# Block-wise matmuls for the last two doubling steps of a triangular inverse

## The chip, the cores and the metric

The kernel runs on one core of a Trainium2 chip, in one launch. Its time is the device time in microseconds (us); each kernel is run several times and the median is compared. The engines named below are TensorE (PE; its weight loads are listed as PEld), VectorE (DVE), ScalarE (ACT), GpSimd (POOL) and the DMA queue of SyncE (SP).

## The reference

A transformer layer over 16 batches of 128 tokens with 512 channels: cross attention to a context of 2048 rows, a gated delta-rule memory layer, and a mixture of 16 experts. The change lies in the second part. For each batch and each of 4 heads (head width 128) the tokens are cut into two chunks of 64, and

```python
strict = jnp.tril(jnp.ones((C, C), bool), -1)
A0 = -jnp.where(strict, jnp.einsum('bnid,bnjd->bnij', wk, wk) * L[:, None], 0.0)
A = jnp.linalg.inv(eye - A0)          # C = 64
...
def step(S, inp):
    v_corr = A_i @ v_i
    wk_corr = A_i @ wk_i
    v_new = v_corr - wk_corr @ S
    o_i = rkg_i @ S + intra_i @ v_new
    S = gamma_C * S + wkg_i @ v_new
```

With two chunks and a state that starts at zero, the kernel treats each head as one 128x128 unit lower triangular system and inverts that.

## The kernel before

One batch after the other goes through the core. A batch's attention is 64 units (4 groups of heads by 16 key blocks), and a unit has two ticks, so a batch has TICKS = 128 ticks. Every engine's program is written out by the same loop over batches `i` and ticks `t`: at each tick it emits a score matmul (L460, every second tick), matmuls whose row maxima are wanted (L447), transposes of the context (L412), products with the values (L472), and the pieces of other batches that the tables place at this tick. So the order on an engine is fixed by hand; an engine that waits holds up everything behind it.

`finish(b, t)` is the part of batch b that comes after its attention and runs while batch b+1 is in attention: output projection, second layer norm, the memory layer, routing. The table `LEVEL_AT` gives three ticks for each of six levels of the inverse. `MT` is the strictly triangular matrix (held transposed, in the buffer x1), `X` the inverse so far (buffer xn2) and `XT` its transpose (buffer xr), each 128x512: four heads side by side. The profile prints these buffers as x, xn and xr. Level lv joins blocks of size s = 2 << lv into blocks of 2s:

- at LEVEL_AT[lv][0] PE computes MT' X into the bank (per head 128x128x128), and DVE copies it to `Y`, masked by a constant `C_LEVEL + lv` that keeps only the s x s blocks that join (L974, buffer Y)
- at LEVEL_AT[lv][1] PE computes Y' XT (per head), and DVE subtracts it from `XT` (L988)
- at LEVEL_AT[lv][2], for all levels but the last, PE transposes XT (L616) and ACT copies it to `X` (L793).

The last level (lv = 5, s = 64) has a form of its own before the change: the helper `joining` multiplies only rows and columns of the 64x64 block (L426), and DVE copies (L979) or subtracts (L988) only that block. Levels 0 to 4 multiply the full 128x128 of each head (L420, helper `per_head`). Every matmul here has 4-byte operands, and the profile lists each of them as two MATMUL records, so four heads are eight records.

Between these steps PE works on attention: L452 transposes the 4 columns of row maxima `mneg` that DVE made in L887. GpSimd adds up the exponentials of every unit (L1094, 60 in a batch) and computes the small reciprocal square roots of the norms (L1097 to L1101); `sums` (L494) needs its additions of a whole batch. The last batch (b = 15) has no attention beside it: its levels are cut into four one-head parts in four banks, and small filler matmuls (L479) stand between its steps.

Of the kernel before, what the change touches and what calls it, by code (L numbers as in the profile page):

```python
# [8 lines left out]
ALU, ACT, AX = mybir.AluOpType, mybir.ActivationFunctionType, mybir.AxisListType  # L9

P = 128
# [6 lines left out]
CH = 64  # L18
# [13 lines left out]
LAST = B - 1  # L32
WARM = {-1: 14, 14: 4}
LEVELS = 6

# [88 lines left out]
def attention(nc, T, w1_first, w1_in):  # L126
    with ExitStack() as ctx:
# [29 lines left out]
        def chunk(b, c):  # L157
# [18 lines left out]
        xr, x1, xn2, x12, rk, V, Y, turned = (  # L176
            sb(n, [P, D]) for n in ("xr", "x1", "xn2", "x12", "rk", "V", "Y", "turned"))
# [3 lines left out]
        XT, MT, X, IT, Vn = xr, x1, xn2, rk, Y  # L181
# [51 lines left out]
        y_dve, xt_dve, x_act = count("y_dve", LEVELS), count("xt_dve", LEVELS), count("x_act", LEVELS - 1)  # L233
# [71 lines left out]
        def heads(ap, n=DH):  # L305
            return ap.rearrange("p (h t) -> p h t", h=n)
# [97 lines left out]
        def _(e):  # L404
# [18 lines left out]
            def joining(out, lhs, rhs, hs):  # L423

                for h in hs:
                    ins = e.matmul(out[:, h, :], lhs[:, h, :], rhs[:, h, :], start=True, stop=True)  # L426
                return ins
# [118 lines left out]
            def finish(b, t):  # L546
# [3 lines left out]
                if t in POST["x1"]:  # L550
# [5 lines left out]
                    ins = project(x1_bank(b), turned, wo, c)  # L556
# [13 lines left out]
                if t in POST["V"]:  # L570
                    ins = project(P_BANK, turned, ww, POST["V"].index(t))
# [19 lines left out]
                for lv in range(LEVELS):  # L591
                    if t == LEVEL_AT[lv][0]:
                        if b == LAST and lv == 0:
                            busy(4)
                        for i, bk, hs in parts:
                            e.wait_ge(*(x_act.at(*level(b, lv - 1, i)) if lv else post_act.at(b, "X1")))
                            if lv < LEVELS - 1:
                                ins = per_head(bk, lambda h: cut(MT, h), lambda h: cut(X, h), hs)
                            else:
                                ins = joining(heads(bk[:])[CH:P, :, 0:CH], heads(MT[:])[0:CH, :, CH:P],  # L600
                                              heads(X[:])[0:CH, :, 0:CH], hs)
                            ins.then_inc(y_pe.sem, 1)
                    if t == LEVEL_AT[lv][1]:
                        for i, bk, hs in parts:
                            e.wait_ge(*y_dve.at(*level(b, lv, i)))
                            if lv < LEVELS - 1:
                                ins = per_head(bk, lambda h: cut(Y, h), lambda h: cut(XT, h), hs)
                            else:
                                ins = joining(heads(bk[:])[0:CH, :, CH:P], heads(Y[:])[CH:P, :, 0:CH],
                                              heads(XT[:])[CH:P, :, CH:P], hs)  # L610
                            ins.then_inc(z_pe.sem, 1)
                    if t == LEVEL_AT[lv][2] and lv < LEVELS - 1:
                        for i, bk, hs in parts:
                            e.wait_ge(*xt_dve.at(*level(b, lv, i)))
                            for h in hs:
                                ins = e.transpose(bk[:, h * P:(h + 1) * P], cut(XT, h), ident)  # L616
                            ins.then_inc(xt_pe.sem, 1)
# [247 lines left out]
        def _(e):  # L865
# [71 lines left out]
            def finish(b, t):  # L937
                banks = banks_of(b)
                w = D // len(banks)
                nh = DH // len(banks)  # L940
# [27 lines left out]
                for lv in range(LEVELS):  # L968
                    if t == LEVEL_AT[lv][0]:
                        for i, bk in enumerate(banks):  # L970
                            cols = slice(i * w, (i + 1) * w)
                            e.wait_ge(*y_pe.at(*level(b, lv, i)))
                            if lv < LEVELS - 1:
                                e.tensor_tensor(  # L974
                                    heads(Y[:, cols], nh), heads(bk[:, cols], nh),
                                    cst[:, C_LEVEL + lv, :].unsqueeze(1).to_broadcast([P, nh, P]), ALU.mult).then_inc(
                                    y_dve.sem, 1)
                            else:
                                e.tensor_copy(heads(Y[:, cols], nh)[CH:P, :, 0:CH],  # L979
                                              heads(bk[:, cols], nh)[CH:P, :, 0:CH]).then_inc(y_dve.sem, 1)  # L980
                    if t == LEVEL_AT[lv][1]:
                        for i, bk in enumerate(banks):
                            cols = slice(i * w, (i + 1) * w)
                            e.wait_ge(*z_pe.at(*level(b, lv, i)))
                            xt, z = XT[:, cols], bk[:, cols]
                            if lv == LEVELS - 1:
                                xt, z = heads(xt, nh)[0:CH, :, CH:P], heads(z, nh)[0:CH, :, CH:P]
                            e.tensor_tensor(xt, xt, z, ALU.subtract).then_inc(xt_dve.sem, 1)  # L988
                if t == POST["x2_add"]:
                    e.wait_ge(*late_pe.at(b, "x2"))  # L990
                    if b:
# [424 lines left out]
```

## Time and profile before

| | |
|---|---|
| time, median of 3 runs | 2172.67 us (2171.48 to 2175.91) |
| time of the profiled execution | 2173.11 us |
| its span | 2171.3 us |
| PE busy | 2095.7 us, 97% |
| POOL busy | 1635.7 us, 75% |
| DVE busy | 1272.3 us, 59% |
| ACT busy | 1220.7 us, 56% |
| mean granted TensorE clock | 0.986 of full speed |

The page gives each engine's busy time and share of the span. A matmul record's end is modelled and reaches past the start of the next one, so PE's 97% does not say that it streams all the time: the distance from one record's start to the next one's is the better measure. The attention part with everything around it lasts to about 1746 us of the span, the experts fill the rest.

### The profile page before, as it was taken

The numbers are of one execution on the slowest core, as the hardware profiler recorded it, in microseconds if no ns is written. First come the engines' busy times: TensorE is split into PE (matmuls) and PEld (weight loads), VectorE is DVE, ScalarE is ACT, GpSimd is POOL, SyncE is SP. The second block draws the span as 40 slices with busy tenths as digits, with TensorE's granted clock in tenths as the row PEclk, the third lists the DMA queues.
The fourth block names the chain that finished last, engine by engine and source line by source line (L and its number), as shares of the span: only waits on it lengthen the run. The fifth ranks groups of instructions, "written<-read, shape, count | busy, mean of one in ns | idle before, by whom it ended". The sixth has DMA issues, their size and how long they took to land. (4 is left out here: it accounts for less than half of the span.)

```text
span 2171.3 us, 35745 instructions
## 1 busy us (share of the span) xinstructions
PE 2095.7 (97%) x12908; PEld 1421.6 (65%) x12908; DVE 1272.3 (59%) x2226; ACT 1220.7 (56%) x2277; POOL 1635.7 (75%) x1387
## 2 busy tenths in 40 slices
PE   7879999999999999999999999999989999999999
PEld 5436565656565656666565656565645789999998
DVE  5656767676666666676767676766664433333332
ACT  3756575666666566666665666666655233433333
POOL 0778888888888888888888888889798145555555
PEclk8989999999999999999999999999999999999999
DMA  4752121212212121212131212112200089999994
GB/s 159 242 113 90 48 74 45 73 52 66 75 48 74 45 73 53 74 44 82 39 97 43 74 43 74 59 57 71 79 15 11 12 313 357 363 352 359 360 348 177
DMA packets 107055, 262.31 MB, mean 121 GB/s; under 512 B 8960, under 2 KB 34304, under 8 KB 98688
## 3 DMA queue, kind: packets, MB, share of 16 engines
q1 hardware_dynamic: 96912, 234.92, 31.6%
q10 hardware_dynamic: 6384, 14.62, 2.3%
q0 software_dynamic: 3584, 10.49, 1.2%
q8 instruction: 103, 1.69, 0.3%
q14 instruction: 72, 0.59, 0.1%
HBM read 223.67 MB, written 25.72 MB: 115 GB/s over the span
## 5 line engine op out<-in xcount | busy, mean ns | idle before, releaser
L1094 POOL TENSOR_TENSOR psum<-psum,weights 128x512 f32<-128x512 f32 x896 | 1152.6, 1286 | 163.4 <-ACT weights L702 60.5
L880 DVE TENSOR_REDUCE mpart<-bank 128x1 f32<-128x512 f32 x1024 | 680.4, 684 | 308.9 <-PE bank L447 300.0
L702 ACT ACTIVATE weights<-bank 128x512 f32<-128x512 f32 x1024 | 597.0, 599 | 324.1 <-PE bank L460 313.3
L460 PE MATMUL bank<-qT,kT 97*128 97x512 f32 x1024 | 482.8, 477 | 10.0 <-DMA qT<-mrow 6.5
L447 PE MATMUL bank<-kT,qT 96*128 96x512 f32 x1024 | 450.0, 451 | 9.6 <-DVE mpart L880 6.8
L447 PEld LDWEIGHTS bank<-kT,qT 96*128 96x128 f32 x1024 | 196.9, 192 | 141.2 <-issue 87.4
L1346 POOL TENSOR_TENSOR w2l<-w,w2h 128x1024 fp32r<-128x1024 f32 x64 | 202.9, 3171 | 75.8 <-PE ebank L1259 54.5
L460 PEld LDWEIGHTS bank<-qT,kT 97*128 97x128 f32 x1024 | 195.7, 193 | 89.4 <-issue 49.2
L472 PE MATMUL bank<-weights,v 128*32 128x512 f32 x2048 | 251.3, 609 | 0.0
L737 ACT COPY w_first<-bank 128x512 f32<-128x512 f32 x248 | 144.7, 584 | 67.6 <-PE bank L412 64.6
L1289 ACT ACTIVATE hh<-ebank 128x512 fp32r<-128x512 f32 x64 | 38.2, 597 | 224.6 <-PE ebank L1243 224.6
L412 PE MATMUL bank<-cst,w_first 128*128 128x128 f32 x992 | 151.5, 276 | 8.3 <-ACT w_first L737 4.7
L412 PEld LDWEIGHTS bank<-cst,w_first 128*128 128x128 f32 x992 | 119.9, 141 | 51.8 <-issue 22.2
L1283 ACT CAST w2h<-w 128x2048 fp32r<-128x2048 f32 x64 | 121.5, 1898 | 43.8 <-DMA w<-in_w 43.8
L472 PEld LDWEIGHTS bank<-weights,v 128*32 128x32 f32 x2048 | 53.7, 110 | 120.2 <-issue 93.8
L538 PE MATMUL bank<-w_first,wkv 128*64 128x512 f32 x512 | 124.0, 605 | 0.0
L1315 DVE SCALAR_TENSOR_TENSOR hl<-ebank,hh 128x512 fp32r<-128x512 f32 x64 | 44.2, 691 | 133.6 <-ACT hh L1289 133.6
L1243 PE MATMUL ebank<-dT,w_first 128*128 128x128 f32 x1024 | 120.2, 278 | 0.9 <-DVE dT L1304 0.9
L1243 PEld LDWEIGHTS ebank<-dT,w_first 128*128 128x128 f32 x1024 | 119.3, 195 | 2.4 <-issue 1.2
L1310 DVE TENSOR_TENSOR w2l<-w,w2h 128x1024 fp32r<-128x1024 f32 x64 | 79.1, 1235 | 71.1 <-PE ebank L1259 48.0
L1243 PEld LDWEIGHTS ebank<-dT,w 128*128 128x128 f32 x1024 | 117.5, 192 | 1.4
L1243 PE MATMUL ebank<-dT,w 128*128 128x128 f32 x1024 | 118.2, 275 | 0.0
(174 smaller groups left out, 3019.3 us busy)
## 6 DMA issues: line engine op xcount, KB each, us to landing
w<-in_w SPq DMA_DIRECT2D x48, 2048.0 KB, 19.9
w_first<-in_ctx SPq DMA_DIRECT2D x62, 1024.0 KB, 5.2
w_first<-in_w SPq DMA_DIRECT2D x16, 2048.0 KB, 12.2
dispatched<-route ACTq DMA_DIRECT2D x17, 513.0 KB, 8.5
dis<-dispatched SPq DMA_DIRECT2D x16, 513.0 KB, 3.5
qT<-qh SPq DMA_DIRECT2D x128, 64.0 KB, 3.4
qT<-qs SPq DMA_DIRECT2D x64, 64.0 KB, 2.1
xr<-in_x SPq DMA_DIRECT2D x16, 256.0 KB, 2.7
```

Source lines behind the costliest of these rows:

```text
L412: ins = e.transpose(out[0:m, j * P:(j + 1) * P], src(j), ident)
L447: e.matmul(a[:], qT[b % 2][0:3 * HD, (4 * g + h) * P:(4 * g + h + 1) * P], kT[b % 2][0:3 * HD, c * 512:(c + 1) * 512], start=True, stop=Tr ...
L460: e.matmul(B_BANK[u % 2][:], kT[b % 2][0:3 * HD + 1, k * P:(k + 1) * P], qT[b % 2][0:3 * HD + 1, g * 512:(g + 1) * 512], start=True, stop= ...
L472: ins = e.matmul(PV_BANK[HD * j:HD * (j + 1), :], v1[b % 2][:, k + j, :], p[(UNITS * b + u + j) % NP], start=k == 0, stop=k == KB - 4)
L538: ins = e.matmul(KV_BANK[rows, :], wkv[:, j, :], cxT[c % 2][:, j, :], start=j < 2, stop=j >= 2)
L702: e.activation(p[n % NP], B_BANK[u % 2][:], ACT.Exp).then_inc(p_act.sem, 1)
L737: e.copy(cxT[c % 2][:, :, kk * P:(kk + 1) * P], turn_bank(b, ("t", k))[:].rearrange("p (c t) -> p c t", c=DC)).then_inc(cxT_act.sem, 1)
L880: e.tensor_reduce(mpart[g % 2][:, 4 * (n % 4) + n // 4:4 * (n % 4) + n // 4 + 1], max_bank(b, g, n)[:], AX.X, ALU.max).then_inc(max_dve.se ...
L1094: e.tensor_tensor(acc[:], first, p[(UNITS * b + u) % NP], ALU.add).then_inc(psum_pool.sem, 1)
L1243: ins = e.matmul(H_BANK[g][:, f * P:(f + 1) * P], w1[q][:, c, (4 * g + f) * P:(4 * g + f + 1) * P], dT[q][:, c, :], start=c == 0, stop=c = ...
L1283: e.copy(w2h[g][:], w2[q][:, 4 * g:4 * g + 4, :]).then_inc(w2h_act.sem, 1)
L1346: e.tensor_tensor(w2l[g % 2][:, 2:4, :], w2[q][:, 4 * g + 2:4 * g + 4, :], w2h[g][:, 2:4, :].bitcast(F32), ALU.subtract).then_inc(w2l_pool ...
```

## The change

Level 4 (s = 32) gets the same treatment as level 5: `joined(lv)` lists the places of the blocks. For level 5 there is one, rows 0 to 63 with 64 to 127, as before. For level 4 there are two, (0 to 31 with 32 to 63) and (64 to 95 with 96 to 127), so each head's 128x128x128 matmul becomes two 32x32x32 matmuls, and each DVE instruction over 128 partitions and 512 columns becomes two over 32 partitions and 4x32 columns. The masked multiply becomes a plain copy. `Y` and `XT` outside the blocks are neither written nor read in these steps. Levels 0 to 3 and the transposes are unchanged. One semaphore increment follows the last of the two, as one followed the single instruction.

```diff
+BLOCKS = 4
+def joined(lv):
+    n = 2 << lv
+    return [(slice(a, a + n), slice(a + n, a + 2 * n)) for a in range(0, P, 2 * n)] if lv >= BLOCKS else []
...
-                            if lv < LEVELS - 1:
+                            if lv < BLOCKS:
                                 ins = per_head(bk, lambda h: cut(MT, h), lambda h: cut(X, h), hs)
-                            else:
-                                ins = joining(heads(bk[:])[CH:P, :, 0:CH], heads(MT[:])[0:CH, :, CH:P],
-                                              heads(X[:])[0:CH, :, 0:CH], hs)
+                            for up, low in joined(lv):
+                                ins = joining(heads(bk[:])[low, :, up], heads(MT[:])[up, :, low],
+                                              heads(X[:])[up, :, up], hs)
...
-                            if lv < LEVELS - 1:
+                            if lv < BLOCKS:
                                 ins = per_head(bk, lambda h: cut(Y, h), lambda h: cut(XT, h), hs)
-                            else:
-                                ins = joining(heads(bk[:])[0:CH, :, CH:P], heads(Y[:])[CH:P, :, 0:CH],
-                                              heads(XT[:])[CH:P, :, CH:P], hs)
+                            for up, low in joined(lv):
+                                ins = joining(heads(bk[:])[up, :, low], heads(Y[:])[low, :, up],
+                                              heads(XT[:])[low, :, low], hs)
...
-                            else:
-                                e.tensor_copy(heads(Y[:, cols], nh)[CH:P, :, 0:CH],
-                                              heads(bk[:, cols], nh)[CH:P, :, 0:CH]).then_inc(y_dve.sem, 1)
+                            for j, (up, low) in enumerate(joined(lv)):
+                                ins = e.tensor_copy(heads(Y[:, cols], nh)[low, :, up],
+                                                    heads(bk[:, cols], nh)[low, :, up])
+                                if j == len(joined(lv)) - 1:
+                                    ins.then_inc(y_dve.sem, 1)
...
-                            if lv == LEVELS - 1:
-                                xt, z = heads(xt, nh)[0:CH, :, CH:P], heads(z, nh)[0:CH, :, CH:P]
-                            e.tensor_tensor(xt, xt, z, ALU.subtract).then_inc(xt_dve.sem, 1)
+                            if lv < BLOCKS:
+                                e.tensor_tensor(xt, xt, z, ALU.subtract).then_inc(xt_dve.sem, 1)
+                            for j, (up, low) in enumerate(joined(lv)):
+                                part = heads(xt, nh)[up, :, low]
+                                ins = e.tensor_tensor(part, part, heads(z, nh)[up, :, low], ALU.subtract)
+                                if j == len(joined(lv)) - 1:
+                                    ins.then_inc(xt_dve.sem, 1)
```

On PE, the order around level 4 of a middle batch, before the change (xn,x are the operands X and MT; xr,Y are XT and Y; the L616 row is the transposes of level 4):

```order
L420 MATMUL bank<-xn,x 128x128 x4
L460 MATMUL bank<-qT,kT 128x512
L452 MATMUL bank<-cst,mneg 128x128
L460 MATMUL bank<-qT,kT 128x512
L447 MATMUL bank<-kT,qT 128x512
L420 MATMUL bank<-xr,Y 128x128 x4
L460 MATMUL bank<-qT,kT 128x512
L447 MATMUL bank<-kT,qT 128x512
L616 MATMUL bank<-cst,xr 128x128 x4
```

And the same place with the change; its lines stand 9 further down in the file:

```order
L435 MATMUL bank<-xn,x 32x32 x8
L469 MATMUL bank<-qT,kT 128x512
L461 MATMUL bank<-cst,mneg 128x128
L469 MATMUL bank<-qT,kT 128x512
L456 MATMUL bank<-kT,qT 128x512
L435 MATMUL bank<-xr,Y 32x32 x8
L469 MATMUL bank<-qT,kT 128x512
L456 MATMUL bank<-kT,qT 128x512
L625 MATMUL bank<-cst,xr 128x128 x4
```

Nothing moved; the two groups of four became groups of eight smaller matmuls, and everything between them is the same. On DVE, the same stretch before (L880 finds row maxima of the L447 matmuls):

```order
L887 TENSOR_REDUCE mneg<-mpart 128x4
L974 TENSOR_TENSOR Y<-bank,cst 128x512
L880 TENSOR_REDUCE mpart<-bank 128x1
L988 TENSOR_TENSOR xr<-xr,bank 128x512
L880 TENSOR_REDUCE mpart<-bank 128x1 x3
L979 COPY Y<-bank 64x4x64
```

And with the change:

```order
L896 TENSOR_REDUCE mneg<-mpart 128x4
L988 COPY Y<-bank 32x4x32 x2
L889 TENSOR_REDUCE mpart<-bank 128x1
L1001 TENSOR_TENSOR xr<-xr,bank 32x4x32 x2
L889 TENSOR_REDUCE mpart<-bank 128x1 x3
L988 COPY Y<-bank 64x4x64
```

Each of the two DVE instructions of level 4 became two, at the same place. ACT, POOL and the DMA queues issue what they issued before, in the same order.

## Rows read from the trace of the kernel before

**Rows 1.** Busy time of each engine in one batch's stretch (window, length, engines, clock, DMA).
```profile
404.80:507.20 102.40, 100.62 (x611) 62.15 (x610) 69.60 (x125) 66.05 (x134) 87.69 (x81) 1.00 0.20 63
```

**Rows 2.** Timeline, PE around level 4 of one batch (start, us, what, idle before).
```profile
431.24 1.16 PE L420 MATMUL bank<-xn,x 128*128 128x128 f32 x8 [0.20 <-ACT xn L793]
...
432.15 0.48 PE L460 MATMUL bank<-qT,kT 97*128 97x512 f32 x1
...
432.50 0.49 PE L460 MATMUL bank<-qT,kT 97*128 97x512 f32 x1
...
432.82 0.40 PE L447 MATMUL bank<-kT,qT 96*128 96x512 f32 x1
...
433.18 1.16 PE L420 MATMUL bank<-xr,Y 128*128 128x128 f32 x8
...
434.10 0.48 PE L460 MATMUL bank<-qT,kT 97*128 97x512 f32 x1
...
434.41 0.40 PE L447 MATMUL bank<-kT,qT 96*128 96x512 f32 x1
...
435.12 0.66 PE L616 MATMUL bank<-cst,xr 128*128 128x128 f32 x4 [0.31 <-DVE xr L988]
```

**Rows 3.** Timeline, DVE in the same stretch.
```profile
431.88 0.17 DVE L887 TENSOR_REDUCE mneg<-mpart 128x4 f32<-128x16 f32 x1
432.44 0.69 DVE L974 TENSOR_TENSOR Y<-bank,cst 128x512 f32<-128x512 f32 x1 [0.39 <-PE bank L420]
433.26 0.69 DVE L880 TENSOR_REDUCE mpart<-bank 128x1 f32<-128x512 f32 x1
434.38 0.69 DVE L988 TENSOR_TENSOR xr<-xr,bank 128x512 f32<-128x512 f32 x1 [0.43 <-PE bank L420]
```

**Rows 4.** Timeline, PE at level 4 of the next batch.
```profile
533.64 1.16 PE L420 MATMUL bank<-xn,x 128*128 128x128 f32 x8 [0.20 <-ACT xn L793]
...
537.52 0.66 PE L616 MATMUL bank<-cst,xr 128*128 128x128 f32 x4 [0.30 <-DVE xr L988]
```

**Rows 5.** Timeline, PE at the first matmuls of level 5, same batch as rows 2.
```profile
436.32 0.39 PE L447 MATMUL bank<-kT,qT 96*128 96x512 f32 x1
436.64 0.67 PE L426 MATMUL bank<-xn,x 64*64 64x64 f32 x8
437.24 0.50 PE L460 MATMUL bank<-qT,kT 97*128 97x512 f32 x1
```

**Rows 6.** Groups by shape: busy us, mean ns of one, idle before.
```profile
L420 PE MATMUL bank<-xn,x 128*128 128x128 f32 x640 | 89.3, 282 | 3.7 <-ACT xn L793 3.2 <-ACT xn L787 0.4
L974 DVE TENSOR_TENSOR Y<-bank,cst 128x128 f32<-128x128 f32 x20 | 4.8, 291 | 5.0 <-PE bank L420 5.0
```

**Rows 7.** One line's instructions, L426: ns min/median/max.
```profile
L426 PE MATMUL bank<-xn,x x128: 218/218/267, 231.9 to 1722.5; 64*64 64x64 f32 x128
```

**Rows 8.** Timeline, DVE at level 4 of the last batch.
```profile
1719.81 0.96 DVE L974 TENSOR_TENSOR Y<-bank,cst 128x128 f32<-128x128 f32 x4 [0.67 <-PE bank L420]
```

**Rows 9.** Timeline, PE, a window 0.06 us long at products with values.
```profile
458.78 0.64 PE L472 MATMUL bank<-weights,v 128*32 128x512 f32 x4
```

**Rows 10.** Timeline, PE at the transposes of level 4, batch 14.
```profile
1655.94 0.66 PE L616 MATMUL bank<-cst,xr 128*128 128x128 f32 x4 [0.55 <-DVE xr L988]
```

**Rows 11.** Timeline, POOL beside level 4, same batch as rows 2.
```profile
430.60 5.52 POOL L1094 TENSOR_TENSOR psum<-psum,weights 128x512 f32<-128x512 f32 x4 [1.19 <-ACT weights L702]
```

**Rows 12.** Timeline, GpSimd's last addition of a batch and the sums that need it.
```profile
462.67 1.27 POOL L1094 TENSOR_TENSOR psum<-psum,weights 128x512 f32<-128x512 f32 x1
...
465.24 0.16 PEld L494 LDWEIGHTS bank<-psum,cst 128*32 128x32 f32 x8 [0.17 <-POOL psum L1094]
```

**Rows 13.** Timeline, POOL at the third norm of one batch.
```profile
451.69 0.19 POOL L1097 TENSOR_TENSOR rs<-mv,eps 128x1 f32<-128x1 f32 x1 [0.30 <-DVE rs L935]
```

**Rows 14.** Timeline, POOL at the second norm of the next batch.
```profile
479.50 1.54 POOL L1094 TENSOR_TENSOR psum<-psum,weights 128x512 f32<-128x512 f32 x1
481.84 0.19 POOL L1097 TENSOR_TENSOR rs<-mv,eps 128x1 f32<-128x1 f32 x1 [0.80 <-DVE rs L935]
```

More of the change, by code:

```diff
@@ L972, in finish @@
                             e.wait_ge(*y_pe.at(*level(b, lv, i)))
-                            if lv < LEVELS - 1:
+                            if lv < BLOCKS:
                                 e.tensor_tensor(
@@ L985, in finish @@
                             xt, z = XT[:, cols], bk[:, cols]
-                            if lv == LEVELS - 1:
-                                xt, z = heads(xt, nh)[0:CH, :, CH:P], heads(z, nh)[0:CH, :, CH:P]
-                            e.tensor_tensor(xt, xt, z, ALU.subtract).then_inc(xt_dve.sem, 1)
+                            if lv < BLOCKS:
+                                e.tensor_tensor(xt, xt, z, ALU.subtract).then_inc(xt_dve.sem, 1)
[4 more added lines that the diff above has]
+                                    ins.then_inc(xt_dve.sem, 1)
                 if t == POST["x2_add"]:
```

## The prediction

> **What bounds the kernel now.** I read the busy times first: PE is busy for 97% of the span. The window of one batch shows the same on a smaller scale [rows 1]: in 102.40 us PE is busy for 100.62, POOL for 87.69, DVE for 69.60, ACT for 66.05, at the full granted clock. The neighbour batch repeats it to the hundredth: its level 4 begins at 533.64 [rows 4], 102.40 us after that of its predecessor at 431.24 [rows 2]. So one stretch of 102.4 us, looked at closely, stands for nearly the whole attention part, and what it loses or saves counts about 14 times.
>
> The second view is the timeline of PE at level 4 [rows 2]. A record's modelled end overlaps the next start, so I read distances of starts. From the first product of level 4 (431.24) to its transposes (435.12) pass 3.88 us. In them PE issues two groups of eight 128x128 records, each followed by the next instruction 0.91 to 0.92 us after it began, and five matmuls of attention. Two places are not filled with work. Two matmuls of 512 columns follow each other 0.31 to 0.34 us apart, but 0.71 us pass from L447 at 434.41 to the transposes at 435.12, and the row names the wait: DVE's subtraction L988. The second group (433.18) starts 0.36 after L447, with DVE's multiply just done at 433.13. In the DVE view [rows 3] the pieces join end to end: PE's first group ends at 432.40, DVE works from 432.44 to 433.13, PE from 433.18 to 434.34, DVE from 434.38 to 435.07, PE goes on at 435.12. Each hand-over costs 0.04 to 0.06 us. So at level 4 this chain, not the sum of PE's work, sets the pace, and all other engines follow PE.
>
> **The change part by part.** It shortens four links of that chain and moves nothing else.
>
> PE's records. Eight 128x128 records last 1.16 us from first start to last end [rows 2]; a record lasts 0.28 [rows 6], so they start (1.16 - 0.28)/7 = 0.126 us apart on average. Level 5's eight 64x64 records last 0.67 us [rows 5], one lasts 0.218 [rows 7], so they start (0.67 - 0.22)/7 = 0.064 us apart. Half the size, half the spacing. No row shows a 32x32 record. From below I bound its spacing by the values products: four 32-column records that use different columns of the array end within 0.64 us of the first start [rows 9], hardly longer than one alone, so issue itself costs next to nothing. From above, by the 0.064 of the nearest shape. The straight line through 128 and 64 columns gives 0.033 for 32, and I take it, since these matmuls halved with size once already. Sixteen records then take 15 x 0.033 = 0.50 from first to last start, and a last record of about 0.19 (0.28, 0.22, then 0.03 to 0.05 less). I add 0.02 for the step to the second block: first start to last end 0.71, against 1.16.
>
> The way out of small tiles. Behind level 5's group L460 starts 0.60 after the first start [rows 5], 0.15 after the last record's start (0.45). So behind 16 small records PE goes on 0.52 + 0.15 = 0.67 after the group's start, against 0.91. The way in: from L447 (436.32) to level 5's group (436.64) are 0.32 us [rows 5], where such a matmul otherwise holds PE for about 0.23; I charge 0.32.
>
> The Trainium skill speaks against the step: TensorEngine Tiling, section Performance Considerations, says that a matmul over 1 column takes as long as one over 60, and TensorE: Matmul & The Clock Gate, section Back-to-back issue gap, gives about 62 ns a matmul where the sequencer's firmware decodes. With the latter the sixteen records would fill 0.99 us and the groups would gain nothing; that is priced as a rival below, from rows. The records of different columns [rows 9] do not agree with such a floor.
>
> DVE. Level 4's multiply and subtraction take 0.69 us each [rows 3]. Two instructions over 4x32 = 128 columns replace each. The trace has them over 128 columns in the last batch: 0.291 us for one [rows 6], and four of them in 0.96 [rows 8], so (0.96 - 0.29)/3 = 0.223 apart. Two take 0.223 + 0.291 = 0.51, 0.18 less. That they use 32 partitions instead of 128 I count as nothing.
>
> Now the new timeline, from the same start 431.24. PE's group ends at 431.95. DVE is not free: L887 ends at 432.05 [rows 3] and stands ahead, so the copies run from 432.08 to 432.60. PE meanwhile goes on at 431.91 with L460, L452, L460 and L447. By the distances of today (0.35 from L460 to L460, 0.32 to L447 [rows 2]) the L447 starts at 432.58 and the second group 0.32 later, at 432.90. DVE's result was there at 432.65, so the wait for DVE is gone and PE's own work decides: 0.28 us gained so far. The second group ends at 433.61. DVE's reduction L880 belongs to L447 and stands ahead of the subtraction; it starts 0.44 after L447 today and lasts 0.69, so it now runs from 433.02 to 433.71. The subtractions follow, until 434.24 at the latest, and PE's transposes start at 434.25 to 434.30, or up to 0.08 earlier if DVE overlaps the two. PE's own work would have allowed 432.90 + 0.67 + 0.33 + 0.23 = 434.13. I take 434.24 against 435.12: **0.88 us less per batch.** So the chain still decides at the transposes, with a wait of 0.1 instead of 0.5.
>
> How often. Batches 0 to 13 have this form (14 x 0.88 = 12.3). Batch 14 has no row maxima beside it and waits even longer for L988 (0.55, [rows 10]): another 0.9. In the last batch each of four one-head parts gets two DVE instructions of 32 columns for one of 128. Four DVE instructions take 0.96 there today [rows 8]; eight short ones, at 0.10 to 0.12 apart, take about as long. PE's first result comes 0.1 to 0.15 earlier and the way to the transposes gets shorter by about 0.3. Sum: 12.3 + 0.9 + 0.3 = 13.5 us.
>
> Is the gain kept? Everything behind is relative to PE's stream, except where POOL falls behind. POOL waits for ACT until 430.60 [rows 11], just ahead of level 4, and then adds without a pause; that start does not move with the saving of its own batch. PE's `sums` need its last addition of the batch, which ends at 463.94; L494 starts at 465.24 [rows 12]. The row names POOL as what it waited for, but POOL had been done for 1.30 us, so that much is spare. The third norm waits 0.30 for DVE [rows 13], and at the second norm of the next batch POOL, busy until 481.04, waits 0.80 [rows 14]: together 1.1 us spare, more than 0.88. After that POOL waits for ACT again. So the gain is kept, with about 0.2 us left before POOL would bind. A gain of 1.2 us or more per batch would not be kept whole.
>
> The sum against the profiled execution: 2173.1 - 13.5 = 2159.6; the median of the runs lies 0.4 under that execution, so **2159.2 us**.
>
> **The rivals.**
> - The spacing does not fall below that of 64x64 (an issue floor). With p the spacing, PE's stream from the first group to the transposes is 30p + 1.9 us (twice 0.15 out, 0.32 in, the attention matmuls 0.35 + 0.32 + 0.33 + 0.23, the rest of the step between blocks). At p = 0.060 to 0.064 that is 3.7 to 3.8, and with the slower chain about 3.75 against 3.88: 0.1 to 0.15 a batch, 2 us in all, 2171. For it: no row shows a smaller record. Against: spacing halved from 128 to 64 columns, and records in different columns start at once.
> - POOL takes part of the gain: if its additions slow, or if the spare at the norms can't be used since ACT needs POOL's result earlier, only 0.3 to 0.6 a batch stays: 2164 to 2168.
> - Slower: small tiles of the same rows and columns can't load weights under a running matmul, so a record costs as long as its 64x64 weight load or more, 0.13 us. Then PE's stream is 30 x 0.13 + 1.9 = 5.8 us against 3.88, 1.9 more per batch, 2201. Breakeven is p = 0.066, and 0.2% slower (0.3 a batch) begins at p = 0.076. Against it: the 64x64 records stand 0.064 apart with four heads on one tile, and a quarter of the array should not be worse.
> - Nothing: the wait moves whole to the next place, such as level 5's first product, which today starts right behind PE's work [rows 5]. It waits for ACT's copy, which follows the transposes and so comes earlier too; I see nothing there that stands still.
>
> **How the numbers follow.** My forecast (0.7 to 1.1 a batch, 2155 to 2163): 0.72. Partly kept, or a spacing between 0.04 and 0.055 (2163 to 2168): 0.12. The floor, or nothing (2168.4 to 2177): 0.10. Slower than that: 0.06. A measurement can tell about 0.2% (4.3 us) from no change. Faster by more 0.84, within it 0.10, slower 0.06. The range for 8 in 10 reaches from 2154, all of POOL's spare used (1.2 a batch), into the partly kept case: 2168.
>
> **What would show it.** In the profile after: 32x32 records at a mean of about 0.19 us, sixteen of them from first to last start in 0.5 us; a distance of about 3.0 us from the first product of level 4 to its transposes in place of 3.88; DVE's copies of 32 partitions right behind L887; batches 101.5 us apart; POOL's wait ahead of the second norm down to about 0.1. I am wrong if the sixteen records take 0.9 us or more, if the distance shrinks and the batches stay 102.4 apart (then look for the engine that the saving ran into, POOL first), or if two DVE instructions over 32 partitions take more than 0.6.

## The result: slightly slower, with its saving visible in the trace

The changed kernel took 2177.25 us (median of 19 runs, 2173.43 to 2181.89), the kernel before 2171.59 beside it (19 runs, 2169.18 to 2179.06). The ratio is 1.0024, with a 95% interval of 1.0016 to 1.0032. The forecast of 2159.2 us and its range to 2168 were wrong. The profiled execution of the changed kernel took 2179.65 us, its span is 2177.8, and its mean granted clock 0.984 (before: 2171.3 and 0.986). Three executions among the runs reported below fell into a disturbed state of 3410 us or more and are left out of their medians.

I start with the page of the kernel after: the busy times, the granted clock in 40 slices, then the window of one batch, which answers to [rows 1].

```profile
PE 2091.4 (96%) x13164; PEld 1410.0 (65%) x13164; DVE 1274.1 (59%) x2264; ACT 1221.7 (56%) x2277; POOL 1636.8 (75%) x1387
...
PEclk8999999999999999999999999999998999999999
```

```profile
401.20:503.60 102.40, 100.02 (x626) 61.36 (x625) 69.47 (x127) 66.10 (x133) 87.73 (x81) 1.00 0.21 63
```

The busy times hardly differ from those before. The clock row has an 8 late in the span (slice 31), where the row before has a 9: PE had less than its full clock there for a while, and I return to it. To see whether the change did what it says, I go to its place. This is the timeline of PE and then of DVE around level 4 in a middle batch after the change (start, us, what, idle before), against [rows 2, 3].

```profile
428.67 0.59 PE L435 MATMUL bank<-xn,x 32*32 32x32 f32 x16 [0.20 <-ACT xn L802]
429.19 0.49 PE L469 MATMUL bank<-qT,kT 97*128 97x512 f32 x1
...
430.26 0.59 PE L435 MATMUL bank<-xr,Y 32*32 32x32 f32 x16
...
431.12 0.40 PE L456 MATMUL bank<-kT,qT 96*128 96x512 f32 x1
...
431.60 0.65 PE L625 MATMUL bank<-cst,xr 128*128 128x128 f32 x4
```

```profile
429.51 0.59 DVE L988 COPY Y<-bank 32x128 f32<-32x128 f32 x2
430.37 0.69 DVE L889 TENSOR_REDUCE mpart<-bank 128x1 f32<-128x512 f32 x1 [0.27 <-PE bank L456]
430.98 0.56 DVE L1001 TENSOR_TENSOR xr<-xr,bank 32x128 f32<-32x128 f32 x2
```

From the first product (428.67) to the transposes (431.60) pass 2.93 us in place of 3.88: 0.95 less. The sixteen records take 0.59 from the first start to the last end. PE no longer waits for DVE ahead of the second group; ahead of the transposes it still does, but less: they start 0.48 after L456 in place of 0.71, 0.06 after the end of DVE's subtractions. Yet the next batch shows the same pace as before:

```profile
531.06 0.31 PE L435 MATMUL bank<-xn,x 32*32 32x32 f32 x4 [0.20 <-ACT xn L802]
```

That is 102.39 us after 428.67; before it was 102.40 [rows 2, 4]. So each batch saves 0.95 us at level 4 and gives it back elsewhere. I followed PE forward from the transposes until the two traces were level again. The place is PE's transposes of the next batch's x, at tick 101 (`xnt` of the table of preparations), just before a batch ends. First the kernel before, not shown so far, then the kernel after: all engines, only the rows that form the chain.

```profile
430.60 9.79 POOL L1094 TENSOR_TENSOR psum<-psum,weights 128x512 f32<-128x512 f32 x7 [1.19 <-ACT weights L702]
...
440.34 0.20 POOL L1097 TENSOR_TENSOR rs<-mv,eps 128x1 f32<-128x1 f32 x1
...
441.24 0.19 POOL L1101 TENSOR_TENSOR rs<-rs 128x1 f32<-128x1 f32 x1
441.41 1.05 PE L420 MATMUL bank<-V,xr 128*128 128x128 f32 x8
441.53 0.81 ACT L717 ACTIVATE xin<-xin,rs 128x512 f32<-128x512 f32 x1
442.40 0.44 PE L412 MATMUL bank<-cst,xin 128*128 128x128 f32 x2
```

```profile
428.04 9.80 POOL L1109 TENSOR_TENSOR psum<-psum,weights 128x512 f32<-128x512 f32 x7 [1.17 <-ACT weights L711]
...
438.69 0.19 POOL L1116 TENSOR_TENSOR rs<-rs 128x1 f32<-128x1 f32 x1
...
438.92 0.81 ACT L726 ACTIVATE xin<-xin,rs 128x512 f32<-128x512 f32 x1 [0.92 <-POOL rs L1116]
439.79 0.66 PE L421 MATMUL bank<-cst,xin 128*128 128x128 f32 x4 [0.83 <-ACT xin L726]
```

Read each block backwards. PE's transposes of xin need ACT's normalisation, that needs POOL's reciprocal square root (three small instructions, L1097 to L1101, after the change L1112 to L1116), and those stand in POOL's queue behind seven additions. The additions began ahead of level 4 (430.60 and 428.04, where ACT still set POOL's pace) and ran without a pause for 9.8 us. So from POOL's first addition to PE's transposes of xin pass 442.40 - 430.60 = 11.80 us before and 439.79 - 428.04 = 11.75 after, whatever PE saves in between. Before, this chain of POOL and ACT and PE's own work arrived nearly together: the group L420 started 0.99 before the transposes, where the like groups of level 4 hold PE for 0.91 to 0.92 [rows 2], and the row names no wait. So there was no time to spare at this place. After, PE stands still for 0.83 us and ACT for 0.92, and the gain is gone. From level 4's transposes to those of xin it is 7.28 us before (435.12 to 442.40) and 8.19 after (431.60 to 439.79): 0.91 of 0.95 given back.

The loss has other places: the last batch and the clock around batches 14 and 15. This is DVE and then PE at level 4 of the last batch after the change (DVE's row before is in [rows 8]).

```profile
1721.41 1.67 DVE L988 COPY Y<-bank 32x32 f32<-32x32 f32 x8 [0.61 <-PE bank L435]
1723.12 1.59 DVE L1001 TENSOR_TENSOR xr<-xr,bank 32x32 f32<-32x32 f32 x8
```

```profile
1721.12 0.68 PE L435 MATMUL bank<-xn,x 32*32 32x32 f32 x16
...
1723.54 1.70 PE L625 MATMUL bank<-cst,xr 128*128 128x128 f32 x4 [0.15 <-DVE xr L1001]
1725.17 1.01 PE L435 MATMUL bank<-xn,x 64*64 64x64 f32 x7
...
1732.41 3.67 PE L425 MATMUL bank<-wr,turned 128*128 128x512 f32 x8
...
1767.28 0.47 PE L1272 MATMUL ebank<-w2h,hh 128*128 128x512 f32 x1 [3.23 <-POOL w2l L1361]
```

And the same place before:

```profile
1719.36 1.08 PE L420 MATMUL bank<-xn,x 128*128 128x128 f32 x8
...
1721.98 0.75 PE L426 MATMUL bank<-xn,x 64*64 64x64 f32 x8
...
1727.38 3.67 PE L416 MATMUL bank<-wr,turned 128*128 128x512 f32 x8
```

Level 4 of the last batch takes 4.05 us after (1721.12 to 1725.17) and 2.62 before. Nothing runs beside it, so DVE sets the pace, and eight small copies take 1.67 where four whole multiplies took 0.96. (The last rows of the two blocks, products with `wr` and, after the change, a product of the experts, serve below.)

Last, windows over stretches at half clock, of before (its second row, at full clock, is the place of a stretch of after) and after (length; busy us of PE, PEld, DVE, ACT, POOL with their instructions; granted clock; DMA share; GB/s).

```profile
1675.20:1682.00 6.80, 6.79 (x28) 3.03 (x27) 1.06 (x6) 2.47 (x8) 6.08 (x6) 0.50 0.00 0
...
1724.00:1731.00 7.00, 6.97 (x40) 4.87 (x39) 0.00 (x0) 1.17 (x2) 0.00 (x0) 1.00 0.00 0
...
1747.00:1757.10 10.10, 8.31 (x37) 7.94 (x38) 0.69 (x1) 0.33 (x1) 0.00 (x0) 0.50 0.95 332
```

```profile
1652.50:1659.00 6.50, 6.50 (x32) 2.39 (x31) 0.43 (x1) 2.51 (x5) 5.26 (x5) 0.50 0.01 3
1672.90:1686.40 13.50, 13.50 (x56) 8.50 (x60) 2.80 (x13) 3.92 (x9) 11.45 (x11) 0.50 0.01 3
...
1724.10:1730.70 6.60, 6.30 (x34) 5.42 (x35) 2.16 (x11) 1.46 (x5) 0.00 (x0) 0.50 0.00 0
...
1768.40:1771.70 3.30, 3.30 (x10) 2.53 (x9) 0.41 (x1) 1.90 (x1) 2.07 (x1) 0.50 1.01 405
```

And PE at the transposes of batch 14's level 4 after, which answers to [rows 10]:

```profile
1651.70 0.66 PE L625 MATMUL bank<-cst,xr 128*128 128x128 f32 x4 [0.23 <-DVE xr L1001]
```

Around the last two batches, before the change, PE is at 0.5 of full speed (the 1.2 GHz level) for one stretch of 6.8 us; after it, for three, 26.6 us together. Where the experts begin it is the other way round: 10.1 us before, 3.3 after.

With these rows the two spans can be reckoned. At the level 4 shown above the kernel after is already 2.57 us ahead (431.24 against 428.67). That can't be put down to the change, since the start of the program takes more or less from execution to execution: three variants of the experiments below, which have whole blocks up to this batch like the kernel before, reach the same place at 429.37, 429.73 and 434.39. At the transposes of batch 14's level 4 the kernel after is 4.24 ahead (1655.94 against 1651.70), and at the last batch's level 4 it is 1.76 behind (1721.12 against 1719.36): 6.0 lost between them, where it has 20.0 us at half clock and the kernel before 6.8. Half of these 13.2 more is 6.6. Level 4 itself costs 1.43 more. From level 5's start to the products with `wr` pass 5.40 before and 7.24 after: 1.84 lost, in the stretch at half clock. From there to the end of the span pass 443.92 (2171.3 - 1727.38) and 445.39 (2177.8 - 1732.41): 1.47 more. -4.24 + 6.0 + 1.43 + 1.84 + 1.47 = 6.5, the difference of the spans.

The 1.47 don't belong to level 4 of the last batch. Two variants below with whole blocks there take 445.4 and 445.7 from the same place to the end, and the variant with small blocks there alone takes 443.7. What differs is where the half clock falls. Before, the stretch of 10.1 us lies where PE waits for the experts' weights in any case: from PE's first instruction of the experts to the first product with w2 pass 14.39 us there (1747.91 to 1762.30), and 14.55 after the change at full clock (1752.73 to 1767.28), the last 3.23 of them a wait. After, the stretch of 3.3 us falls on products that nothing holds up: they start 0.43 apart in it and 0.23 outside.

### The profile page after: what moved, and what is told of

Its sections match the earlier page's. It is cut to its first block and busy times, and to the rows that moved or that the text cites. A ratio compares the mean times of both kernels' runs of the same rounds, so it can differ in the third digit from the quotient of the medians.

```text
span 2177.8 us, 36295 instructions
## 1 busy us (share of the span) xinstructions
PE 2091.4 (96%) x13164; PEld 1410.0 (65%) x13164; DVE 1274.1 (59%) x2264; ACT 1221.7 (56%) x2277; POOL 1636.8 (75%) x1387
## 5 line engine op out<-in xcount | busy, mean ns | idle before, releaser
L456 PE MATMUL bank<-kT,qT 96*128 96x512 f32 x1024 | 448.8, 449 | 9.7 <-DVE mpart L889 6.7
L456 PEld LDWEIGHTS bank<-kT,qT 96*128 96x128 f32 x1024 | 196.5, 192 | 140.4 <-issue 88.0
```

Source lines behind the costliest of these rows:

```text
L456: e.matmul(a[:], qT[b % 2][0:3 * HD, (4 * g + h) * P:(4 * g + h + 1) * P], kT[b % 2][0:3 * HD, c * 512:(c + 1) * 512], start=True, stop=Tr ...
```

## The experiments

My theories after the result: **A**, POOL's backlog at the first norm of the next batch takes the gain of the middle batches. **B**, in the last batch, two DVE instructions for one cost time, and the clock follows. The rivals: the small matmuls themselves cost PE something elsewhere, or the gain is bounded by another engine than POOL. Every run stands beside runs of the kernel before on the same chip.

### Which batches carry the loss

Two kernels, in which `joined` and the tests on `BLOCKS` depend on the batch:

```diff
-BLOCKS = 4
+def blocks(b):
+    return 4 if b < LAST else 5      # e1_not_last
+    return 5 if b < LAST else 4      # e2_last_only
```

Of the first, the small blocks in batches 0 to 14, was expected:

> The small blocks at level 4 for batches 0 to 14 only; the last batch keeps the full 128x128 products and the single DVE instructions. Theory A (the 0.95 us that a middle batch gains at level 4 is given back 5 us later, where PE's transposes of the next batch's x wait for ACT, and ACT for POOL; the loss of the whole change comes from the last batch): 0 to 3 us below the kernel before, batches 102.4 us apart. Rival B (the loss comes from the middle batches or batch 14, whose PE works less and loses clock): 4 to 7 us above the kernel before, as the whole change. Rival C (a mere difference between builds, such as the start of the run): no relation to which batches are changed.

Of the second, the small blocks in the last batch alone:

> The small blocks at level 4 in the last batch only. Theory A: 4 to 7 us above the kernel before; level 4 of the last batch takes about 4.1 us from its first product to level 5's first in place of 2.6, and a stretch at half clock follows it. Rival B: within 1.5 us of it, the 1.5 us of the longer level 4 alone at most.

Measured beside 2174.64 for the kernel before (23 runs): the first 2175.26 (11 runs), ratio 0.9997 [0.9989, 1.0006]; the second 2178.54 (12 runs), ratio 1.0017 [1.0008, 1.0026]. So the change in fifteen batches together comes to nothing that can be told from zero (the interval is about 2 us to either side), and most of the loss is that of the one last batch. What the profile of the kernel after lost around batch 14 does not appear in the median of the first kernel, though its own profiled execution, the slowest of the eleven (2178.42), has stretches of 6.7 and 13.5 us there too. In the second kernel DVE's eight copies in the last batch take 1.67 us, as in the kernel after, and level 4 takes 4.05. A stretch at half clock comes here too, as level 4 ends:

```profile
1726.30:1733.00 6.70, 6.39 (x36) 5.98 (x37) 1.61 (x8) 1.09 (x3) 0.00 (x0) 0.50 0.00 0
```

From level 5's start (1726.72) to the products with `wr` (1734.28) pass 7.56 us in place of 5.40. So 1.43 for level 4 and 2.16 for the clock behind it make 3.6; the timed runs lose 3.9 (2178.54 against 2174.64).

### Moving the place where the gain is lost

If the wait for POOL's norm takes the gain, a later place for what needs it should set the gain free. In the table of preparations (ticks relative to the batch's start) I moved ACT's normalisation and PE's transposes seven ticks back, with the change and without it:

```diff
-STEADY = Prep(norm=-32, xn=-29, xnt=-27,
+STEADY = Prep(norm=-32, xn=-22, xnt=-20,
```

> The changed kernel, with ACT's normalisation of the next batch's x moved 7 ticks later (xn -29 to -22) and PE's transposes of it with it (xnt -27 to -20), so that POOL's backlog has some 5 us more before anyone waits for it. Theory A: the 0.95 us per middle batch stays: batches 101.5 us apart, 12 to 13 us less in the middle than in the kernel with the same move and without the small blocks (next run), so with the last batch's loss 6 to 9 us less than it in all. Rival D (PE's stream or another link fixes 102.4): batches stay 102.4 apart in both.

> The kernel before with the same two table entries moved. Theory A: about as the kernel before, 0 to 3 us less (the 0.1 us that PE waits there per batch goes), batches 102.3 to 102.4 apart. Rival D: the same. If this alone gains 10 us, the wait at x was worth more than I read and level 4 was bound by it both ways.

Measured: with the change 2190.56 (6 runs, 2181.23 to 2198.79), ratio 1.0079 [1.0054, 1.0104]; without it 2190.26 (5 runs, 2188.16 to 2192.04), ratio 1.0072 [1.0059, 1.0085]. The move is bad in itself: without the change it was expected to cost nothing, and it costs 15.6 us. At the new place PE waits for ACT anyway, as the row without the change shows:

```profile
449.39 0.66 PE L412 MATMUL bank<-cst,xin 128*128 128x128 f32 x4 [1.07 <-ACT xin L717]
```

Batches are 103.55 us apart without the change and 102.55 with it, so under the same move the change is worth 1.00 us per batch, and the profiled spans are 2188.0 and 2179.4. The medians are equal all the same, where 6 to 9 us less were expected: three of the six executions with the change took 2181 to 2184 us at a mean clock of 0.982, the other three 2197 to 2199 at 0.973 to 0.975. The saving is there, and the clock takes it back in half of the executions. These two runs support A by the distances of their batches, not by their times.

### Giving POOL's norm an earlier place

The better edit leaves ACT and PE where they are and puts the statistics and POOL's three small instructions four ticks earlier, ahead of more of its additions. One number changes, again with the change and without:

```diff
-STEADY = Prep(norm=-32, xn=-29, xnt=-27,
+STEADY = Prep(norm=-36, xn=-29, xnt=-27,
```

> The changed kernel with one table entry moved: the statistics and GpSimd's reciprocal root of the next batch's x come 4 ticks earlier (norm -32 to -36), which puts GpSimd's three small instructions ahead of two of its additions; ACT's and PE's parts stay where they were. Theory A (the gain is given back because PE's transposes of x wait for ACT and ACT for POOL's backlog): PE no longer waits there, and batches are 101.4 to 101.7 us apart in place of 102.4. The tail's loss stays, and clock may be lost more often. Rival D (something else than POOL fixes 102.4): 102.4 as before.

> The kernel before with the same entry moved. Theory A: batches 102.3 to 102.4 apart, since PE waited for only 0.1 us there, and a time within 3 us of the kernel before. Rival D: the same here; what tells is the difference to the run above, 0.8 to 1.0 us per batch by theory A, none by D.

Measured beside 2174.20 (34 runs): with the change 2168.83 (10 runs), ratio 0.9981 [0.9966, 0.9996]; without it 2172.19 (10 runs), ratio 1.0003 [0.9989, 1.0017]. These two runs decide A. The same edit is worth nothing to the kernel before, where PE arrived together with POOL's chain, and it releases the gain in the kernel after. The rows, with the change in a later batch (POOL, ACT and PE, then the x transposes of the next batch), and without it:

```profile
529.02 6.96 POOL L1109 TENSOR_TENSOR psum<-psum,weights 128x512 f32<-128x512 f32 x5 [1.18 <-ACT weights L711]
...
536.83 0.19 POOL L1116 TENSOR_TENSOR rs<-rs 128x1 f32<-128x1 f32 x1
539.07 0.81 ACT L726 ACTIVATE xin<-xin,rs 128x512 f32<-128x512 f32 x1
539.93 0.66 PE L421 MATMUL bank<-cst,xin 128*128 128x128 f32 x4
...
641.49 0.66 PE L421 MATMUL bank<-cst,xin 128*128 128x128 f32 x4
```

```profile
542.14 0.66 PE L412 MATMUL bank<-cst,xin 128*128 128x128 f32 x4
...
644.55 0.44 PE L412 MATMUL bank<-cst,xin 128*128 128x128 f32 x2
```

POOL's small chain now stands behind five additions instead of seven and ends 2.05 us before ACT starts with it, and neither ACT nor PE waits. With the change the batches are 101.56 us apart (641.49 - 539.93), without it 102.41. The difference, 0.85 a batch, is what I had forecast (0.88) as the change's own gain. No other engine took it back: the rival that something else than POOL bounds the batch falls.

### The early norm without the last batch, and without the last two

The small blocks in batches 0 to 14, with norm=-36, and then in batches 0 to 13 (`4 if b < LAST - 1 else 5`), which leaves out batch 14 as well:

> Small blocks for batches 0 to 14, the last batch as before, and norm 4 ticks earlier: both causes of loss taken away. Theory A: 10 to 13 us less than the kernel before when the clock holds, 2160 to 2166. If the clock falls in more of the executions (as in half of those of the run with x moved 7 ticks), the times spread over 10 us or more and the median is worse.

> Small blocks for batches 0 to 13 only, norm 4 ticks earlier. Theory G (the small blocks of batch 14, where no row maxima fill PE, are what makes the half clock after it last 13.7 us in place of 6.8): 6.8 us of half clock there and 3 us less than the run with batches 0 to 14, 2160 or so. Rival H (the length of that stretch follows from the phase at which the attention ends, not from batch 14's blocks): 13.7 us again, and the same time as that run.

The first: 2162.99 (11 runs, 2161.42 to 2167.91), ratio 0.9959 [0.9946, 0.9971]. Without the last batch the kernel with the early norm gains another 5.8 us (2168.83 to 2162.99), somewhat more than the price of that batch alone (3.9). The second: 2161.41 (6 runs, 2159.79 to 2166.86) beside 2172.29 (16 runs), ratio 0.9953 [0.9938, 0.9969]. It is the fastest version measured, ahead of both kernels; its lead over the first is within the intervals, as the two were timed beside different runs of the kernel before.

Their profiles (spans 2161.2 and 2158.0) differ in the clock around batch 14. A window of the first, and one of the second:

```profile
1661.20:1674.70 13.50, 12.85 (x56) 8.50 (x60) 2.81 (x13) 4.70 (x11) 11.92 (x12) 0.50 0.01 1
```

```profile
1660.10:1666.70 6.60, 6.60 (x31) 3.45 (x29) 1.06 (x6) 2.95 (x7) 5.88 (x6) 0.50 0.00 0
```

With small blocks in batch 14 the half clock lasts 13.5 us, with whole ones 6.6, worth up to about 3.4 us. From level 4 of batch 14 to that of the last batch pass 69.4 us in the first (1640.30 to 1709.74) and 67.2 in the second (1637.35 to 1704.57). The spans differ by 3.2, but other stretches of the two differ as well.

### The last batch: how much is DVE's number of instructions?

The small blocks in the last batch only, where the four copies to `Y` become one masked multiply over 128 partitions each, as before the change (the rest of the bank holds old values, which the mask takes out); the subtraction keeps its two instructions per head:

```diff
+                            one = b == LAST and lv == 4
-                            if lv < blocks(b):
+                            if lv < blocks(b) or one:
                                 e.tensor_tensor(
...
-                            for j, (up, low) in enumerate(joined(b, lv)):
+                            for j, (up, low) in enumerate([] if one else joined(b, lv)):
```

> As the run with the small blocks in the last batch alone, but there DVE writes Y in one masked instruction over all 128 partitions, as before the change, in place of two copies. Theory E (two DVE instructions on different partitions follow each other at 0.2 us each and don't overlap, so a head costs 0.43 us in place of 0.22): the four heads' Y takes 0.96 us again in place of 1.7, and level 4 of the last batch (its first product to level 5's first) takes about 3.3 us in place of 4.1. Rival F (PE's small records make level 4 long): 4.1 as before.

```profile
1717.69 0.89 DVE L985 TENSOR_TENSOR Y<-bank,cst 128x128 f32<-128x128 f32 x4 [0.61 <-PE bank L436]
1718.49 1.58 DVE L1003 TENSOR_TENSOR xr<-xr,bank 32x32 f32<-32x32 f32 x8
```

Measured: 2174.36 (10 runs, 2169.8 to 2179.58), ratio 1.0007 [0.9992, 1.0022]. Level 4 of the last batch falls from 4.05 to 2.99 us: 1.06 less for one instruction in place of two, at the same number of small matmuls. The row of `Y` falls as well (0.89 for four against 1.67 for eight), that of the subtractions keeps its 1.58. So DVE's second instruction for `Y`, and not PE's small matmuls, accounts for 1.06 of the 1.43 us. The half-clock stretch behind it stays (clock 0.50 from 1720.60 to 1727.20). The interval holds both no change and the loss of about 3 us that the profile would give, so on the time this run doesn't decide.

### Batch 14 alone

> Small blocks at level 4 in batch 14 alone, the norm entry as before. Theory G: 13.7 us of half clock after batch 14 and 2 to 3 us above the kernel before. Rival H: 6.8 us as in the kernel before, and within 1 us of it.

Measured: 2175.87 (10 runs, 2169.01 to 2200.95), ratio 1.0017 [0.9991, 1.0044]: unclear as a time. Its profile has both stretches that the kernel after has around batch 14:

```profile
1653.90:1660.50 6.60, 6.60 (x30) 2.45 (x28) 0.43 (x1) 2.18 (x5) 5.66 (x5) 0.50 0.00 0
1674.40:1688.00 13.60, 13.43 (x56) 8.63 (x60) 2.78 (x13) 4.22 (x10) 11.59 (x12) 0.50 0.01 1
```

And it does not have the third, behind the last batch's level 4, which keeps whole blocks here (clock 1.00 from 1724.00 to 1731.00). Over all twelve profiles that third stretch goes with the last batch's blocks without an exception: the five kernels with small blocks there have it (after, last batch alone, late transposes, early norm, one instruction for `Y`), the seven with whole ones don't. The stretch of 13.5 us goes with batch 14's small blocks in five of six kernels. The sixth is the changed kernel with the late transposes. Its blocks in batch 14 are small, and it has full clock from 1652.4 to 1679.7 and then no more than the kernel before:

```profile
1679.80:1686.50 6.70, 6.69 (x28) 3.06 (x28) 1.06 (x6) 2.37 (x7) 5.98 (x6) 0.50 0.00 0
```

From batch 14's level 4 to the last batch's it takes 66.8 us (1657.17 to 1723.95), against 72.1 in the kernel after and 67.3 before. So small blocks in batch 14 alone don't make the long stretch; what stands around them counts too, and the theory that it follows from the blocks is not shown. All this is one profiled execution of each kernel.

## Why the prediction was wrong

**The matmuls of 32x32: right.** Two terms were forecast from the neighbours, the spacing (0.033 us) and the record (about 0.19). Groups of the kernel after by shape (busy us, mean ns of one, idle before):

```profile
L435 PE MATMUL bank<-xr,Y 32*32 32x32 f32 x256 | 9.8, 194 | 0.7 <-DVE Y L988 0.5
...
L988 DVE COPY Y<-bank 32x128 f32<-32x128 f32 x30 | 8.7, 290 | 0.7
...
L988 DVE COPY Y<-bank 32x32 f32<-32x32 f32 x8 | 1.5, 190 | 0.8 <-PE bank L435 0.6
```

A record lasts 0.194, sixteen last 0.59 together, so they start (0.59 - 0.19)/15 = 0.027 apart. PE goes on 0.52 after the group's start (forecast 0.67: 0.12 of the difference are the spacing, 0.03 the way out). The floor of about 62 ns a matmul that was weighed as a rival does not show. The Trainium skill, TensorE: Matmul & The Clock Gate, section Back-to-back issue gap, also has a floor of about 25 ns for 1 to 64 columns, where the sequencer's firmware is not in the way; 27 ns for these records agrees with that, and the 64 ns of the 64x64 records doesn't.

**DVE's pair: mis-sized.** Two copies of 32 partitions take 0.59 us, two subtractions 0.56, against 0.51. A copy lasts 0.290, so the second starts 0.30 after the first, with the end of it, where 0.223 was forecast from instructions over all 128 partitions. In the middle batches this cost at most 0.05: PE's second group starts 0.16 after the copies' end and doesn't wait for them, and only the transposes wait for the subtractions.

**The distance at level 4: right.** 2.93 us against about 3.0, and the chain of the new timeline holds link by link: copies behind the reduction, no wait before the second group, and the transposes right behind the subtraction. (Six matmuls of attention stand in that stretch, not five: L452 was not counted, but the distances used hold it.)

**"Is the gain kept?": here the prediction failed.** It named four meetings of PE and POOL (`sums`, the third norm, the second norm, the start ahead of level 4), found spare time of 1.30, 0.30 and 0.80, and concluded that the gain is kept. The first norm of the next batch, at ticks 96 to 101, was not among them. It lies 6 to 8 us behind level 4's transposes, POOL comes to it straight from seven additions, and its spare time was nothing. The sentence "that start does not move with the saving of its own batch" was right, and it held the loss: what POOL does from that start on lasts 11.8 us up to PE's transposes, and PE could not come out of them earlier. The third norm's wait of 0.30 was added to the second's as spare, though neither stands between the saving and this place. Shown by the pair with norm=-36: 102.41 to 101.56 us a batch with the change, and 2168.83 against 2172.19.

**"How often": the last batch was mis-sized.** Eight short DVE instructions were taken as long as four (0.96), at 0.10 to 0.12 apart. They took 1.67 and 1.59: the level cost 1.43 more instead of 0.3 less. The run with one instruction for `Y` gives 1.06 of it back. As far as the rows tell, the term that failed is the one that the prediction counted as nothing, that the pair uses sets of 32 partitions; no run varies that alone. Short instructions on the same partitions do start before the former ends, as level 5's copies in the last batch of the kernel before show:

```profile
1722.34 0.65 DVE L979 COPY Y<-bank 64x64 f32<-64x64 f32 x4 [0.68 <-PE bank L426]
```

Each of these lasts 0.22 to 0.23, so they start (0.65 - 0.23)/3 = 0.14 apart. The copies of 32x32 last 0.190 and start 0.21 apart, each behind the end of the former. Added to this came a stretch at half clock that the prediction had no term for: 1.84 us up to the products with `wr`.

**The rivals.** "Nothing: the wait moves whole to the next place" was the right one for the middle batches, and shared a chance of 0.10 with the floor after a look at level 5 only. "POOL takes part of the gain" (0.12, shared) named the right engine and even the link ("ACT needs POOL's result earlier"), but looked for it at the norms that had spare time and priced it at a part, 0.3 to 0.6 kept, where 0.04 was kept. The slower rival had another mechanism (a weight load per record), and that one is refuted. The prediction also named the sign that came, a shorter distance with batches 102.4 apart, and POOL as the first place to look. Adding up: 14 x 0.88 forecast, about nothing measured (ratio 0.9997 without the last batch); batch 15 forecast at -0.3, measured at +3.9.

**What stays open.** In four of the six kernels with small blocks in the middle batches one middle batch of the profile takes 104.5 to 105.7 us, with a half-clock stretch of 6.8 in it: at 428.3 and 428.9 with the early norm, at 739.4 in the kernel without the last batch's small blocks, at 1461.3 with the late transposes. None of the six with whole blocks there has one. Nor is it a matter of the profiled executions alone: the mean clock of the timed ones is 0.983 in the middle for the kernel after (0.981 to 0.985), and with the early norm 0.9825 with the change against 0.987 without it. That can account for the time of the early norm. 14 x 0.85 = 11.9 us less were to be had against the same kernel without the change, level 4 of the last batch takes 1.4 of it, and the medians differ by 3.4 (2172.19 and 2168.83). The 7 us between are an estimate of what the clock took: 0.0045 of 2170 us are 19.5 us more at half clock, worth at most 9.8. I have no experiment that says when the clock falls. And whether batch 14's small blocks cost anything in the timed runs is left unclear by their interval.

## What to carry to other kernels

Before a saving is counted once per loop, follow the helper engines' chains through the whole period and write down the spare time at every place where the main engine waits for one of them, above all where small work stands in an in-order queue behind a saturated one: a place that shows no wait may have no spare time either, and what its engine began ahead of the saving doesn't move. A chain like this is opened by moving the small work ahead in the queue, not by moving its reader. Splitting a DVE instruction over partitions costs next to nothing where another engine is late anyway, and costs in full where nothing runs beside it, so such a change is judged (and made) per place: here the batches with attention beside them gain with it once the norm has moved, and the last one doesn't.

## What the runs showed of the hardware

- Successive DVE instructions overlapped on the same partitions and not between different ones. Of 128 columns each, two over all 128 partitions start 0.223 us apart though one lasts 0.291 [rows 6, 8], and two over different sets of 32 partitions start 0.30 apart at a length of 0.290. Of 64x64 on the same partitions they start 0.14 apart at 0.22 to 0.23, and of 32x32 on alternating sets 0.211 apart ((1.67 - 0.19)/7) at 0.190. So a head of the last batch pays 0.42 us for its pair, and one whole instruction 0.223: a quarter of the partitions and a quarter of the columns saved 0.10 of an instruction's length and 0.01 of its distance to the next.
- Records of 32x32 with 4-byte operands start 0.027 us apart beside attention, 64x64 ones 0.064 [rows 5, 7], and 128x128 ones 0.126 [rows 2, 6]. In the last batch it is 0.033 for 32x32 ((0.68 - 0.19)/15) and 0.114 for 128x128 ((1.08 - 0.28)/7).
- Shorter matmuls in the same schedule came with a lower granted clock in places: in the profiled executions 26.6 us at half clock around batches 14 and 15, in place of 6.8, and in the timed ones a mean clock of 0.983 in the middle (0.981 to 0.985) where the kernel before, in the runs beside the experiments, has 0.986 or 0.987 (0.984 to 0.990). Time saved on PE's path is not all time won, if the clock answers.
- What half clock costs depends on the place: 10.1 us of it at the beginning of the experts, where PE waits for weights in any case, cost nothing that the rows show, and behind the last batch's level 4 a stretch of 6.6 to 6.7 cost 1.84 and 2.16 us.
